# Products of three dense taps in one VectorE operation, and a gathered unit's last addition moved to TensorE

## The reference, cut to what matters

```python
for dy in (0.0, 1.0):
    for dx in (0.0, 1.0):
        iy = y0 + dy
        ix = x0 + dx
        wgt = (1.0 - jnp.abs(py - iy)) * (1.0 - jnp.abs(px - ix))
        ...
        g = jax.vmap(lambda xb, ib: jnp.take(xb, ib, axis=1))(xf, idx.reshape(B, -1))
        acc = acc + wgt[:, None] * g.reshape(B, C, 9, H, W)
...
z = jnp.einsum('bckhw,ock->bohw', cols, w_dcn.reshape(O, -1, 9)) + b_dcn[None, :, None, None]
```

## Time and profile before

| what | us |
|---|---|
| median of 3 runs | 6852.37 |
| lowest, highest | 6847.77, 6854.86 |
| the profiled execution: time | 6857.4 |
| the profiled execution: span | 6855.5 |
| busy in the span: PE, DVE, ACT, POOL | 6015.5, 4827.7, 2206.7, 4622.6 |
| mean granted TensorE clock | 0.912 of full speed |

### The profile page before, as it was taken

One profiled execution on the slowest core, in us unless ns is written; L12 is line 12 of the kernel. 1 busy time (PEld: TensorE's weight loads), 2 busy tenths in 40 slices (PEclk: granted clock), 3 DMA queues, 4 the chain that ended last, 5 costly groups with the idle time before them and its releaser, 6 DMA issues. The chain is left out here.

```text
span 6855.5 us, 125468 instructions
## 1 busy us (share of the span) xinstructions
PE 6015.5 (88%) x47333; PEld 4757.1 (69%) x47333; DVE 4827.7 (70%) x11440; ACT 2206.7 (32%) x3376; POOL 4622.6 (67%) x4765
## 2 busy tenths in 40 slices
PE   6987988887988988888887898899999989998996
PEld 6886776756776766676754665577777767776775
DVE  7887787866777867777864555467767766676675
ACT  1212222232222232222222322244444444443442
POOL 0005776667777767777767777767777777777776
PEclk9997998988999988999987888899999999998998
DMA  4223333324333323333322222233323323332332
GB/s 149 98 97 115 99 102 104 111 87 130 104 102 103 111 88 98 100 106 96 111 80 77 82 71 67 85 87 92 89 81 104 95 79 99 92 91 78 93 83 75
DMA packets 364107, 653.44 MB, mean 95 GB/s; under 512 B 112008, under 2 KB 270744, under 8 KB 355608
## 3 DMA queue, kind: packets, MB, share of 16 engines
q0 software_dynamic: 152064, 311.73, 16.4%
q1 hardware_dynamic: 211480, 333.92, 15.6%
HBM read 599.16 MB, written 46.15 MB: 94 GB/s over the span
## 5 line engine op out<-in xcount | busy, mean ns | idle before, releaser
L882 POOL DMA_INDIRECT G<-table,IDX x4752 | 4608.5, 970 | 2186.8 <-issue 1929.4
L2247 DVE TENSOR_TENSOR ARENA<-ARENA,OUT 128x288 f32<-128x288 f32 x2808 | 1056.9, 445 | 101.0 <-PE RED L1107 70.8
L1107 PE MATMUL RED<-IDENT,ARENA 128*96 128x128 f32 x7344 | 887.1, 280 | 80.6 <-DVE ARENA L2247 80.2
L1498 ACT ACTIVATE SAMP<-RED 96x384 f32<-96x384 f32 x688 | 334.6, 486 | 1902.0 <-PE RED L1316 814.2
L2062 DVE TENSOR_TENSOR G<-G,WPS 128x1152 f32<-128x1152 f32 x528 | 711.1, 1347 | 297.8 <-DMA G<-table,IDX 296.5
L1107 PEld LDWEIGHTS RED<-IDENT,ARENA 128*96 128x96 f32 x7344 | 819.2, 130 | 133.5 <-issue 122.7
L1297 PE MATMUL BTP<-PAD,ARENA 80*128 x2304 | 751.8, 450 | 57.8 <-issue 32.4
L1059 PE MATMUL OFF<-PAD,ARENA 128*54 128x128 f32 (+1 forms) x10944 | 752.6, 296 | 21.3 <-ACT PAD L1398 15.4
L1176 PE MATMUL BTP<-X 80*128 80x480 f32 x1248 | 650.0, 639 | 135.5 <-ACT X L1442 67.7
L1493 ACT ACTIVATE SAMP<-RED 96x384 f32<-96x384 f32 x528 | 256.9, 487 | 1559.1 <-PE RED L1195 680.4
L1059 PEld LDWEIGHTS OFF<-PAD,ARENA 128*54 128x54 f32 (+1 forms) x10944 | 670.6, 134 | 121.6 <-issue 98.1
(11 more groups left out here) (213 smaller groups left out, 7688.4 us busy)
## 6 DMA issues: line engine op xcount, KB each, us to landing
ARENA<-wtab SPq DMA_DIRECT2D x208, 800.0 KB
G<-table,IDX POOLq DMA_INDIRECT x4752
ARENA<-xo SPq DMA_DIRECT2D x96, 720.0 KB
X<-xo SPq DMA_DIRECT2D x80, 360.0 KB
table<-TB SPq DMA_DIRECT2D x64, 384.0 KB, 2.6
X<-x SPq DMA_DIRECT2D x3, 3200.0 KB, 19.9
out<-X SPq DMA_DIRECT2D x20, 320.0 KB
wtab<-TB SPq DMA_DIRECT2D x16, 384.0 KB, 2.5
```

Of the source, the lines that this page charges most:

```text
L882: pool.indirect_dma_start(G[:, b, k, :], None, tables[seg.table], bass.IndirectOffsetOnAxis(ap=IDX[:, q, b * TAPS + k:b * TAPS + k + 1], a ...
L1107: last = nc.tensor.matmul(RED[b % 2][0:TPG * C, gr * 128:(gr + 1) * 128], PROD[gr][:, sft, :], IDENT[:, :], start=(sft == 0), stop=(sft == ...
L1498: nc.scalar.activation(SAMP[:, x], RED[x][0:TPG * C, 0:GROUPS * 128].rearrange("p (g n) -> p g n", g=GROUPS), ACT.Copy).then_inc(z.samp_re ...
L2247: last = nc.vector.tensor_tensor(out=PROD[gr][:, :, j * C:(j + 1) * C].rearrange("p (dy dx) c -> p dy dx c", dy=3), in0=win[:, gr:gr + 3, ...
```

## The change

It has two parts.

**Dense products.** The table `wtab` is now laid out image by image: an entry is 32 floats of one image, there are four images one after the other, and a window is loaded by two transfers (one for each image of the pair), each with pieces of 5 x 32 floats (RUN was 320 floats and is 160). The total of bytes stays the same. In such a window the three horizontal neighbours are 96 adjacent floats, so the three taps of a group are one operation with three-dimensional patterns, 864 products, in place of three of 288. It is used in all dense units (x and d).

**The last addition in C1.** In gathered units of C1, `halve` writes its 576 sums to PARTS instead of back into G, and signals `summed` itself; `sum_up` is gone. TensorE transposes both halves and adds them in PSUM, two matmuls for each group. PARTS is SUM for even units and 576 floats of ARENA for odd ones. C2 keeps `halve` and `sum_up`.

```diff
-RUN = SH * R2
+RUN = SH * C
...
+        PARTS = [SUM, arena(1620, 2 * TAPS * C).rearrange("p (s k c) -> p s k c", s=2, k=TAPS)]
...
             def window(seg, i, tt):
-                first = seg.p % 2 * WENT + tt * 128 + 1
-                tiles = bass.AP(wtabs[seg.p // 2], first * R2, [[256 * R2, DENSE], [R2, 128], [PW * R2, SH], [1, RUN]])
-                sp.dma_start(WIN[tt][:, :, :], tiles[bass.ds(i, 1)].rearrange("n p d f -> (n p) d f")).then_inc(win_loaded[tt], 16)
+                for im in range(2):
+                    first = (seg.p % 2 * 2 + im) * WENT + tt * 128 + 1
+                    tiles = bass.AP(wtabs[seg.p // 2], first * C, [[256 * C, DENSE], [C, 128], [PW * C, SH], [1, RUN]])
+                    sp.dma_start(WIN[tt][:, im, :, :], tiles[bass.ds(i, 1)].rearrange("n p d f -> (n p) d f")).then_inc(win_loaded[tt], 16)
...
+                def add_parts(red, b):
+                    for gr in range(GROUPS):
+                        for part in range(2):
+                            last = nc.tensor.matmul(red[0:TPG * C, gr * 128:(gr + 1) * 128],
+                                                    PARTS[b % 2][:, part, TPG * gr:TPG * (gr + 1), :].rearrange("p k c -> p (k c)"),
+                                                    IDENT[:, :], start=(part == 0), stop=(part == 1), is_transpose=True)
+                    last.then_inc(main.reduced, 1)
...
                 def turn_beside(step, b):
                     pe.wait_ge(main.summed, UNITS * step.i + b + 1 + UNITS)
                     pe.wait_ge(main.samp_ready, step.v + 2 * b + 1)
-                    for gr in range(GROUPS):
-                        last = nc.tensor.transpose(RED[0][0:TPG * C, gr * 128:(gr + 1) * 128],
-                                                   SUM[:, b % 2, TPG * gr:TPG * (gr + 1), :].rearrange("p k c -> p (k c)"),
-                                                   IDENT[:, :])
-                    last.then_inc(main.reduced, 1)
+                    on.add_parts(RED[0], b)
...
+                def part(m, b):
+                    g = G[:, b]
+                    dve.wait_ge(main.scaled, UNITS * m + b + 1)
+                    dve.wait_ge(main.reduced, UNITS * m + b + 1)
+                    nc.vector.tensor_tensor(out=PARTS[b % 2][:, :, :, :], in0=g[:, :, 0:2 * C].rearrange("p k (s c) -> p s k c", s=2),
+                                            in1=g[:, :, 2 * C:].rearrange("p k (s c) -> p s k c", s=2), op=ALU.add).then_inc(main.summed, 1)
...
                         on.scale(main, m, step.q, b)
-                        on.halve(main, m, b)
-                        on.sum_up(main, m, b)
+                        on.part(m, b)
...
                 def weight_window(step, b, gr):
-                    win = WIN[b // 2][:, :, :].rearrange("p y (x c) -> p y x c", c=R2)[:, :, :, b % 2 * C:(b % 2 + 1) * C]
                     dve.wait_ge(prod_used, step.wg + (GROUPS if step.drain and b == 0 else 3 * b + gr + 1))
-                    for j in range(TPG):
-                        w9 = W9[step.q][b // 2][:, b % 2 * TAPS + TPG * gr + j, :].rearrange("p (dy dx) -> p dy dx", dy=3)
-                        last = nc.vector.tensor_tensor(
-                            out=PROD[gr][:, :, j * C:(j + 1) * C].rearrange("p (dy dx) c -> p dy dx c", dy=3),
-                            in0=win[:, gr:gr + 3, j:j + 3, :], in1=w9.unsqueeze(3).to_broadcast([128, 3, 3, C]), op=ALU.mult)
-                    last.then_inc(prod, 1)
+                    corner = WIN[b // 2][:, b % 2, gr, 0:C]
+                    win = bass.AP(corner.tensor, corner.offset, [list(corner.ap[0]), [C, TPG], [RUN, 3], [1, 3 * C]])
+                    first = b % 2 * TAPS + TPG * gr
+                    w9 = W9[step.q][b // 2][:, first:first + TPG, :].rearrange("p j s -> p (j s)")
+                    nc.vector.tensor_tensor(out=PROD[gr].rearrange("p (dy dx) (j c) -> p j dy dx c", dy=3, j=TPG), in0=win.rearrange("p j dy (dx c) -> p j dy dx c", dx=3), in1=w9.rearrange("p (j dy dx) -> p j dy dx", j=TPG, dy=3).unsqueeze(4).to_broadcast([128, TPG, 3, 3, C]), op=ALU.mult).then_inc(prod, 1)
```

More of the change, by code:

```diff
@@ L651, in table_block @@
             np_ = columns(i)
+            if windows:
+                to = TB[i % NTB][0:np_, :, :].rearrange("p b (im j c) -> p (b im) j c", im=2, j=BT)
+                return (to[:, :, half * 3:(half + 1) * 3, :],
+                        BTP[half][0:np_, 0:6 * R2].rearrange("p (j b c) -> p b j c", j=3, b=IMG))
             to = TB[i % NTB][0:np_, :, half * 3 * R2:(half + 1) * 3 * R2]
-            j = 3 if windows else 6
-            return (to.rearrange("p b (j c) -> p b j c", j=j),
-                    BTP[half][0:np_, 0:6 * R2].rearrange("p (j b c) -> p b j c", j=j, b=2))
+            return (to.rearrange("p b (j c) -> p b j c", j=6),
+                    BTP[half][0:np_, 0:6 * R2].rearrange("p (j b c) -> p b j c", j=6, b=2))
         block = ctx.enter_context(nc.Block())
@@ L1090, in consume @@
                         pe.wait_ge(z.samp_ready, step.v + b + 1)
-                        for gr in range(GROUPS):
-                            last = nc.tensor.transpose(RED[b % 2][0:TPG * C, gr * 128:(gr + 1) * 128],
-                                                       SUM[:, b % 2, TPG * gr:TPG * (gr + 1), :].rearrange("p k c -> p (k c)"),
-                                                       IDENT[:, :])
-                        last.then_inc(z.reduced, 1)
+                        if z is main and step.seg.s == C1:
+                            on.add_parts(RED[b % 2], b)
+                        else:
+                            for gr in range(GROUPS):
+                                last = nc.tensor.transpose(RED[b % 2][0:TPG * C, gr * 128:(gr + 1) * 128],
+                                                           SUM[:, b % 2, TPG * gr:TPG * (gr + 1), :].rearrange("p k c -> p (k c)"),
+                                                           IDENT[:, :])
+                            last.then_inc(z.reduced, 1)
                         if b == 2:
@@ L2143, in consume @@
                         on.scale(z, m, step.q, b)
-                        on.halve(z, m, b)
-                        on.sum_up(z, m, b)
+                        if z is main and seg.s == C1:
+                            on.part(m, b)
+                        else:
+                            on.halve(z, m, b)
+                            on.sum_up(z, m, b)
                         if b == 1:
@@ L2186, in consume_both @@
                         on.weight_half(half, im, 6)
-                        on.halve(main, m, b + 1)
+                        on.part(m, b + 1)
                         on.weight_half(half, im, 7)
-                        on.sum_up(main, m, b + 1)
                         on.weight_half(half, im, 8)
@@ L2221, in consume_pair @@
                         if b % 2 == 0:
-                            dve.wait_ge(win_loaded[b // 2], 16 * (d + 1))
+                            dve.wait_ge(win_loaded[b // 2], 32 * (d + 1))
                         on.scale(main, m, step.q, b)
-                        on.halve(main, m, b)
-                        on.sum_up(main, m, b)
+                        on.part(m, b)
                         if b == 1:
```

22 lines of the change are left out of this document (11 added, 11 removed).

## The result

| | before | after |
|---|---|---|
| median, us (4 runs each) | 6853.61 | 6731.61 |
| lowest to highest | 6847.77 to 6862.40 | 6723.98 to 6732.48 |
| ratio, 95% interval | 1 | 0.9819 (0.9804 to 0.9833) |
| span of the profiled execution | 6855.5 | 6729.8 |
| mean granted TensorE clock | 0.912 | 0.928 |

The change made the kernel 122 us faster. The forecast was 74 us faster, 6778, in a range from 6745 to 6824: right in direction, outside the range, more won than forecast.

The account below looks back on a forecast made before the run. TensorE was taken to bound stage A, chains of VectorE and TensorE the mixed stage, gathers C1 of pair 3. Terms -102 - 4 - 5 + 31 + 6 = -74 gave 6778 us against the median, range 6745 to 6824.

Parts of the forecast that it names:

- The x steps: Mixed stage: earlier unit 2 sum and full clock behind TensorE's wait; 3.1 us in 33 steps, 1.4 in three, -106 us.
- The f steps: Mixed stage, TensorE-bound: 12 extra turns add 1.3 us to each of 24 steps, 31 us lost.
- The d steps: Mixed stage: cheaper dense products win 0.12 us per step (0 to 1.6), 5 us over 42 steps.
- g steps: Mixed stage: g steps wait on gathers, so the change brings 0.
- C1 of pair 3: Bound by gathers, so 0; up to 21 us if the extra turns show.
- Gathers late at the pairs' starts, +6: Starts of pairs: 45.5 us of gathers a tile against 45.0 for an x and a d step; 6 us added.
- B: Rival, x steps: the half-clock stretches stay, saving only 24 us, 6828; chance 0.12.
- D: Rival, dense products: one operation of 864 has a pitch of 1.40 us, +220 us, 7072; chance 0.07.
- E: Rival, mixed stage: smaller window pieces make each gather 5% longer to issue, taking the gain back, 6850; chance 0.08.
- C: Rival: long x stretches return 3.4 us, f's extra turns lie partly in its waits; -105, 6747; chance 0.13.
- A: Main forecast for the whole kernel: 74 us less, own range 6760 to 6800; chance 0.60.
- the prediction's bound: Stage A: with half-size window pieces the DMA share of 0.32 at most doubles to 0.64.

Follow-up runs that it names:

- e_u01: The changed kernel, with products in units 2 and 3 of the x steps as three operations of 288 again; 6745.2 us, ratio 0.9837 to before.
- e_u23: The changed kernel, with products in units 0 and 1 of the x steps as three operations of 288 again; 6753.1 us, ratio 0.9847 to before.
- e_fill: The kernel before, with 24 idle turns on TensorE in each x step ahead of its wait for unit 2's sum; 6801.4 us, ratio 0.9932.
- e_products: The kernel before with the dense part alone (table by image, one operation of 864), last addition still on VectorE; 6786.0 us, ratio 0.9908.
- e_join: The changed kernel, but in f steps VectorE adds the two halves of PARTS and TensorE makes single turns; 6720.3 us, ratio 0.9798 to before.
- e_xparts: The changed kernel, with f steps wholly back to halve and sum_up with single turns; 6723.5 us, ratio 0.9813 to before.
- e_table: The kernel before with the table and windows laid out by image alone, three operations of 288, last addition on VectorE; 6853.1 us, ratio 1.0005.
- e_parts: The changed kernel with three operations of 288 in every dense unit; table by image and PARTS stay; 6794.4 us, ratio 0.9924 to before.
- the repeat: The changed kernel itself measured once more, nothing altered; 6726.4 us, ratio 0.9818 to before.
- the last version: The changed kernel with halves added on VectorE in f steps and idle turns behind every x step; 6713.6 us, ratio 0.9787; once more, 6708.6, 0.9785.

## Why the prediction was wrong, point by point

- **The x steps: right in mechanism, in size partly by luck.** -106 was forecast, -109.9 came, and each time inside the step of the earlier trace rows is within 0.2 us. e_u01 and e_u23 show that only work ahead of unit 2's sum counts, e_fill that the clock alone is worth 1.65 us a step as the mean of 36, e_products that it does not come back by the dense part alone. But two errors cancel: of the 33 x steps with a stretch in the middle, the 21 with one of 3.4 us gained 3.00 us each (forecast 3.1), and the 12 with one of 6.8 us gained 3.95; the other three, forecast to gain 1.4 each, gained nothing in sum. The sum also leaves out an operation of VectorE between the first two units (the 0.42 us of `finish`, L2232 after): the units end at 10.56 and not at 9.94. It cost nothing, since TensorE turned the offsets for `locate` at the same time.
- **The f steps: right.** +31 was forecast, +28.0 came; e_join and e_xparts give most of it back by undoing the turns.
- **The d steps: the step that failed.** I wrote that TensorE leaves 0.2 us open per unit, and then took "0.12 us per step". Four units make 0.8 us a step, 34 us in 42 steps, against 5 taken. e_products shows 29.3 us, with undisturbed d steps of 15.3 in place of 15.9 us (0.6 x 42 = 25), the rest by the clock (12 half-clock starts for 16). The trace had it: VectorE was busy 15.01 of a d step's 15.92 us and TensorE 14.60 at full clock. In the full change 22 to 25 us of it remain, because of the next point.
- **The d steps' clock: not seen.** The same half-clock stretch that I found behind the wait in the x steps also lies at the start of d steps, where TensorE waits for the first products: 3.76 us in 6 of the 16 before, which stand behind f steps, and 1.96 to 2.21 us in the other 10, behind x steps. The prediction treated d steps as all at full clock. Here is one of these 10 (windows of an undisturbed one, with a wait of 2.17 us, and of it, with 2.20; the granted clock is the third number from the right):

```profile
764.08:780.00 15.92, 14.60 (x152) 13.62 (x153) 15.01 (x44) 2.90 (x8) 12.06 (x13) 1.00 0.35 107
1048.17:1065.61 17.44, 16.11 (x152) 15.14 (x153) 15.11 (x45) 2.86 (x8) 13.21 (x14) 0.90 0.32 102
```

  When an x step's middle keeps the clock, the start of a d step loses it more often. With products of 288 in the d steps, the d steps with such a start are 16 and 15 where the middles lose the clock (before, e_table), and 25 and 27 where they mostly keep it (e_fill, e_parts). With products of 864 they are 12 in e_products and 13 to 19 in the kernels whose x steps keep it and that have no idle turns (19 and 17 in the two executions of the change). Such a d step is 16.9 us for 15.3.
- **G freed earlier: costed at nothing.** I had `summed` moved to `halve` among the edits and gave it no term, and g steps 0. They gained 11.3 us (10.5 in the repeat, 12.5 in e_join, but 1.8 in e_xparts, where the f steps ahead of them free G late as before). So it is the f steps' earlier release that pays in the g steps. The traces show where: in the g steps of pairs 1 and 2 VectorE waited 5.8 and 6.3 us for G before, not at all after, and 7.4 and 7.5 us in e_xparts. C1 of pair 3 gained 3 to 8 us in five kernels with the earlier release, but 0 to 3 in those that join the halves, and e_table without it gained 3.8: there it is not shown.
- **Gathers late at the pairs' starts, +6: wrong for this kernel.** VectorE waited 9.7 us for G, not more than before. More of such waits came one step further on, in e_join (35 us) and with idle turns (91 us).
- **The rivals.** B (the stretches stay) and D (a slow 864) fall by the rows above. E falls too: a gather takes 966 ns for 970, and e_table has the smaller pieces and takes the same time as the kernel before. C was nearest in size (6747 against 6732), but its reasons carry little of it: the f steps' turns were not hidden, and the longer stretches gave 0.95 us more in 12 steps, 11 us.
- **The rule of the Trainium skill** ("TensorE: Matmul & The Clock Gate", "Part 4: PE-mode transpose") that turns by the transpose mode do not engage the full clock: the runs disagree again. In e_fill 24 turns of the identity, and nothing else, kept the clock at 1.00 through a wait behind which it had fallen to 0.50 in 33 of 36 steps.

Sum: -109.9 - 21.6 + 28.0 - 11.3 - 6.4 = -121 in C1, against -74. Of the 47 us between, 17 are the d steps, 11 the g steps, 6 the late gathers, 6 pair 3, 4 the x steps and 3 the f steps. All erred the same way, and the range was too narrow for it: the text gives a d step 0 to 1.6 us, which is up to 67 us in 42 steps, but the range of A allows for nothing but 0.6 us either way in the x steps, and the g steps had no bound at all.

## What to carry to other kernels

Where a step is a chain that changes engines, cost each edit by whether it lies before or behind the hand-over, and count the slack per unit times the units. A clock that falls behind a wait is part of a wait's price: look for every place with such a wait, since here curing one made the next one likelier. And write beside every gain how much idle time the next engine has left; here the last version gave back 10 of 18 us in steps where VectorE then waited for gathers.

## What the runs showed of the hardware

- The granted clock fell to 0.50 behind every wait of TensorE of 3.16 to 3.38 us in the middle of x steps (before; also behind two of 1.69 and 1.78 in steps that had begun at half clock), behind 24 of 30 waits of 2.59 to 3.00 (e_products) and behind 8 waits of 2.08 to 2.15 in e_parts, where it stayed behind others of the same length, one of them shown above. It stayed at 1.00 behind all of 1.10 to 1.39 there (after). At the start of d steps it fell behind waits of 1.96 and 2.20 us and stayed behind another of 2.17; after the change it fell behind nine waits of 1.83 us and stayed behind eleven of the same length. So the length of one wait doesn't decide alone; what else does, these runs don't settle.
- Window pieces of half the size cost little: queue q1, which carries the windows, had 67% more packets, and they took 11% more time in sum (17.6% of 16 engines over 6729.8 us against 15.6% over 6855.5). The DMA share of a step of stage A went from 0.32 to 0.36, where the prediction's bound was 0.64.

```profile
q0 software_dynamic: 152064, 311.73, 18.7%
q1 hardware_dynamic: 352856, 333.94, 17.6%
```

- The packets of the gathers (q0) took 118 ns each in the profiled execution before (0.164 x 16 x 6855.5 / 152,064) and 132 ns after. It is not the windows' pieces that make the difference: e_fill loads its windows in whole pieces as before and has 130 ns (the line below, over 6797.1 us), and e_table, with the halved pieces alone, has 130 ns too. What made them faster in that one execution stays open. GpSimd's instruction was 970, 967 and 966 ns in before, e_table and after.

```profile
q0 software_dynamic: 152064, 311.73, 18.2%
```
